# A graph network's joined node pass: ScalarE's copy of turned rows moved between the halves of the next item's normalization, and TensorE's product behind the base product

## The chip, the cores and the metric

The kernel runs on one core of a Trainium2 chip. The metric is the device time of one execution in microseconds, the median of a few runs. The core has TensorE (PE, matrix products into PSUM), VectorE (DVE), ScalarE (ACT), GpSimd (POOL) and SyncE (SP); DMAs are issued here from SP, ScalarE and GpSimd and run on 16 DMA engines. Each engine runs its own program in order, and the programs meet only at semaphores.

## What is computed

There are 100000 nodes of 128 features and 50000 edges, sorted by their destination. Two residual blocks follow each other, each on `relu(layernorm(x))`:

```
h = relu(layernorm(x))
x = x + relational_conv(h)          # 16 relations out of 8 bases, summed over the edges into dst, + h_bias
h = relu(layernorm(x))
g = leaky(h @ enc_w + enc_b)        # leaky(v) = v or 0.1 v
for l in 0, 1:
    agg = segment_sum(g[src], dst) / max(degree, 1)
    g = leaky(agg @ lin_l_w[l] + lin_l_b[l] + g @ lin_r_w[l])
x = x + g
```

All of it is float32.

## The kernel before

The kernel makes four passes, one after the other: a relational pass over the edges, the node pass, and one pass for each of the two layers. The change is in the node pass alone (`node_pass`, L985). It computes the new `x`, its layer norm, the encoder's `g`, and of layer 0 the two parts that need no exchange between nodes: the base `g @ w_r + bias` for every node, and for every edge the row of `g` at its source, summed over equal destinations within the sorted edges and multiplied by `w_l`.

The pass walks 294 items, in a repeating order of three: two blocks of 512 nodes and one tile of 512 edges. For edges the rows of `x` at the source come from a copy that the pass before laid out by edge, and the rows of the aggregate are gathered with indirect DMAs. I call three items a beat; there are 98.

One item goes through these steps:
- SP loads `first` and `term` (L1106 to L1110) into a ring of 12 slots. GpSimd gathers `term` for edges (L1075) and scatters the finished rows (L1084), each with four indirect DMAs a beat.
- VectorE adds the two (L1299), takes statistics (L1304) and, once a beat, the variance of 12 groups (L1314 to L1324). ScalarE takes the square root, `deviation` (L1233). VectorE makes `rstd` and `shift` from it (L1332, L1334).
- ScalarE normalizes with `normalize(n, lo, hi)` (L1244): four instructions of 128 columns, called in two halves, (0, 2) and (2, 4). Only the second half signals that `h` is complete.
- TensorE turns the four 128x128 pieces (`turn`, L1158) into a PSUM bank; ScalarE copies the turned rows to SBUF (`keep_turned`, L1254).
- TensorE multiplies by `enc_w` (`product`): for a block one product that leaves features on the partitions (L1179), for edges the bias and four products (L1171, L1175).
- ScalarE makes a tenth of the product (`tenth`, L1264 for blocks, L1261 for edges), and VectorE takes the maximum of product and tenth (`leaky`, L1349 for blocks, L1343 for edges).
- For blocks TensorE computes the base (`base_product`, L1187 and L1191), ScalarE evicts it (`keep_base`, L1271), and SP stores it (L1130). For edges TensorE sums runs (`sum_runs`, L1202), VectorE carries the sums on (L1380), TensorE multiplies by `w_l` (`to_rows`, L1211) and VectorE scales the rows (`finish`, L1389).

The order of the work is written out by hand, as one loop over n on each engine, in which each step works at an item some places back. The lag of a step is the same on both sides of the change. `ht_ps`, `g_ps`, `z_ps`, `h`, `ht`, `tmp` and `g_t` have two buffers each. The waits that matter here: `keep_turned(n)` waits for `turn(n)`; `product(n)` waits for `keep_turned(n)` and for the maximum of item n-2, whose bank it takes; `tenth(n)` waits for `product(n)`; `base_product(n)` and `sum_runs` wait for the maximum of their item; `keep_base` waits for its base product; `turn(n)` waits for the second half of `normalize(n)`.

In iteration n TensorE has this order: product of item n-1, run sums or base product of item n-3, row product of item n-5 (if it is a tile of edges), turn of item n. ScalarE has: the deviation if a beat is about to begin, copy of n-1, tenth of n-2, first half of the normalization of n, base eviction of n-4 (if it is a block), second half of n. VectorE has: carried sums of n-4, addition and statistics of n+4, the variance, the scales of the next beat, the maximum of n-2, and the comparisons and the scaling of rows for edges.

Of the kernel before, what the change touches and what calls it, by code (L numbers as in the profile page):

```python
# [68 lines left out]
def gnn_kernel(nc, x, src, dst, etype, basis_w, w_comp, h_bias, enc_w, enc_b, lin_l_w, lin_l_b,  # L69
# [20 lines left out]
    with ctx:  # L90
# [894 lines left out]
        def node_pass():  # L985

            X_TILES = 4
            ITEMS = 3 * (T // X_TILES)
# [7 lines left out]
            with ExitStack() as st:  # L996
# [54 lines left out]
                def block_of(n):  # L1051
                    return n // 3 * 2 + n % 3

                def valid(n, edges):
                    return 0 <= n < ITEMS and is_edges(n) == edges
# [9 lines left out]
                with nc.Block() as block:  # L1065
# [85 lines left out]
                    @block.tensor  # L1151
                    def _(pe):
                        def turn(n):
                            pe.wait_ge(s_h, n + 1)
                            if n >= 2:
                                pe.wait_ge(s_ht, n - 1)
                            for j in range(NB):
                                last = nc.tensor.transpose(ht_ps[n % 2][:, j * P:(j + 1) * P],  # L1158
                                                           h[:, n % 2, j * P:(j + 1) * P], ident[:])
                            last.then_inc(s_turn, 1)  # L1160

                        def wait_g_bank(n):

                            if n >= 0:
                                pe.wait_ge(s_leaky, n + 1)

                        def product(n):
                            pe.wait_ge(s_ht, n + 1)
                            wait_g_bank(n - 2)
                            if is_edges(n):  # L1170
                                nc.tensor.matmul(g_ps[n % 2][:], ones_bf[0:96, :],  # L1171
                                                 bias_parts[0:96, 0, :].unsqueeze(1).to_broadcast([96, NB, P]),
                                                 start=True, stop=False)
                                for j in range(NB):
                                    last = nc.tensor.matmul(g_ps[n % 2][:, j * P:(j + 1) * P],  # L1175
                                                            ht[:, n % 2, j * P:(j + 1) * P], w_enc[:],
                                                            start=False, stop=(j == NB - 1))
                            else:
                                last = nc.tensor.matmul(g_ps[n % 2][:], w_enc[:], ht[:, n % 2, :], start=True, stop=True)  # L1179
                            last.then_inc(s_g, 1)  # L1180

                        def base_product(n):
                            d = block_of(n)
                            pe.wait_ge(s_leaky, n + 1)
                            if d >= 2:
                                pe.wait_ge(s_kept, d - 1)
                            nc.tensor.matmul(z_ps[d % 2][:], ones_bf[0:96, :],  # L1187
                                             bias_parts[0:96, 1, :].unsqueeze(1).to_broadcast([96, NB, P]),
                                             start=True, stop=False)
                            for j in range(NB):  # L1190
                                last = nc.tensor.matmul(z_ps[d % 2][:, j * P:(j + 1) * P],  # L1191
                                                        g_t[:, d % 2, j * P:(j + 1) * P], w_r[:, 0, :],
                                                        start=False, stop=(j == NB - 1))
                            last.then_inc(s_z, 1)

                        def sum_runs(i):
                            pe.wait_ge(s_leaky, 3 * i + 3)
                            pe.wait_ge(s_same, i + 1)
                            if i:
                                pe.wait_ge(s_carried, i * X_TILES)  # L1200
                            for j in range(X_TILES):
                                last = nc.tensor.matmul(sum_ps[:, j * P:(j + 1) * P], g_rows[:, i % 2, j * P:(j + 1) * P],  # L1202
                                                        same[:, i % 2, j, :], start=True, stop=True)
                            last.then_inc(s_summed, 1)

                        def to_rows(i):
                            pe.wait_ge(s_carried, (i + 1) * X_TILES)
                            if i:
                                pe.wait_ge(s_rows, i)
                            for j in range(X_TILES):  # L1210
                                last = nc.tensor.matmul(row_ps[:, j * P:(j + 1) * P], sums[:, j, :], w_l[:, 0, :],  # L1211
                                                        start=True, stop=True)
                            last.then_inc(s_rowed, 1)

                        for n in range(ITEMS + 6):
                            if 1 <= n <= ITEMS:
                                product(n - 1)
                            if valid(n - 3, True):
                                sum_runs((n - 3) // 3)
                            if valid(n - 3, False):  # L1220
                                base_product(n - 3)
                            if valid(n - 5, True):
                                to_rows((n - 5) // 3)
                            if n < ITEMS:
                                turn(n)

                    @block.scalar
                    def _(act):
                        def deviation(b):
                            act.wait_ge(s_var, b + 1)  # L1230
                            if b >= 2:
                                act.wait_ge(s_rstd, b - 1)
                            nc.scalar.activation(std[:, b % 2, :], var[:, b % 2, :], ACT.Sqrt).then_inc(s_std, 1)  # L1233

                        def normalize(n, lo, hi):
                            b, k = n // 3, n % 3
                            if lo == 0:
                                act.wait_ge(s_shift, b + 1)
                                act.wait_ge(s_base, n + 1)
                                if n >= 2:  # L1240
                                    act.wait_ge(s_turn, n - 1)
                            for j in range(lo, hi):
                                c = k * NB + j
                                last = nc.scalar.activation(h[:, n % 2, j * P:(j + 1) * P],  # L1244
                                                            base[:, n % SLOTS, j * P:(j + 1) * P], ACT.Relu,
                                                            bias=shift[:, b % 2, c:c + 1], scale=rstd[:, b % 2, c:c + 1])
                            if hi == NB:
                                last.then_inc(s_h, 1)
# [7 lines left out]
                        def tenth(n):  # L1256
                            act.wait_ge(s_g, n + 1)
                            if n >= 2:
                                act.wait_ge(s_leaky, n - 1)
                            if is_edges(n):  # L1260
                                nc.scalar.activation(tmp[:, n % 2, :], g_ps[n % 2][:], ACT.Copy,  # L1261
                                                     scale=SLOPE).then_inc(s_tenth, 1)
                            else:
                                nc.scalar.activation(tmp[:, n % 2, :], g_ps[n % 2][:], ACT.Identity, bias=tenth_col[:],  # L1264
                                                     scale=SLOPE).then_inc(s_tenth, 1)
# [8 lines left out]
                        for n in range(-1, ITEMS + 4):  # L1274
                            if (n + 1) % 3 == 0 and n + 1 < ITEMS:
                                deviation((n + 1) // 3)
                            if 1 <= n <= ITEMS:
                                keep_turned(n - 1)
                            if 0 <= n - 2 < ITEMS:
                                tenth(n - 2)  # L1280
                            if 0 <= n < ITEMS:
                                normalize(n, 0, 2)
                            if valid(n - 4, False):
                                keep_base(block_of(n - 4))
                            if 0 <= n < ITEMS:
                                normalize(n, 2, NB)

# [670 lines left out]
```

## Time and profile before

| | us |
|---|---|
| median of 3 runs | 3753.05 (3751.85 to 3756.4) |
| the profiled execution, its own time | 3751.84 |
| its span, first to last instruction | 3749.7 |
| VectorE busy | 3011.4 (80%) |
| GpSimd busy | 2473.7 (66%) |
| TensorE matmuls busy | 2432.4 (65%) |
| ScalarE busy | 1879.4 (50%) |
| mean granted clock of TensorE | 0.894 of full |

The profile is of one execution. The normalization instructions of the node pass start between 1239.4 and 2384.8 us, so this pass takes a bit under a third of the span. In the rows below "idle before" in brackets is how long the engine stood before the instruction, and behind the arrow is what released it. A PE line is a matrix product, PEld the loading of its weights. The end of a matrix product is modelled. Durations of neighbouring instructions on one engine overlap, so the distance from start to start is the better price of an instruction.

### The profile page before, as it was taken

The page shows a single profiled execution, that of the slowest core. Times are in us where ns is not written, and L with a number is a line of the kernel's source. Part 1 is how long each engine was busy: PE and PEld are TensorE (multiplying, and loading weights), DVE is VectorE, ACT ScalarE, POOL GpSimd, SP SyncE. Part 2 cuts the span into 40 slices and gives each one's busy share as a digit, 9 for nine tenths or more (in the row PEclk, how much of TensorE's full clock was granted, in tenths as well). Part 3 has the DMA queues.
Part 4 walks back from the last instruction along what each step waited for, and adds up shares of the span by engine and source line. Part 5 has one row for each costly group of instructions (what it writes and reads, how often), then busy time and mean ns, then how long its engine had stood idle before and what let it go on. Part 6 is the DMA issues. An engine that isn't in the chain of part 4 may idle for free. (4 is left out here: it accounts for less than half of the span.)

```text
span 3749.7 us, 58608 instructions
## 1 busy us (share of the span) xinstructions
PE 2432.4 (65%) x13938; PEld 1774.0 (47%) x13938; DVE 3011.4 (80%) x8321; ACT 1879.4 (50%) x4979; POOL 2473.7 (66%) x2363
## 2 busy tenths in 40 slices
PE   1679999999998577777777777477778871000000
PEld 0445555555554466665565566377777771000000
DVE  3479999999998788888888888688888884555565
ACT  0346666666665577777777777345445541000000
POOL 0357777777776567666666666576666654677665
PEclk9989999999999899999999999799999995555555
DMA  8776666666662888888888888399999997999998
GB/s 277 312 235 205 203 201 209 206 209 207 208 198 65 274 254 259 262 263 265 265 265 266 268 267 249 133 346 388 389 383 385 388 370 300 416 416 416 415 410 319
DMA packets 664350, 1065.77 MB, mean 284 GB/s; under 512 B 74065, under 2 KB 379651, under 8 KB 657586
## 3 DMA queue, kind: packets, MB, share of 16 engines
q1 hardware_dynamic: 486572, 599.67, 49.5%
q10 hardware_dynamic: 95904, 305.70, 20.4%
q0 software_dynamic: 81536, 156.64, 13.0%
q8 instruction: 121, 1.98, 0.2%
q14 instruction: 217, 1.78, 0.1%
HBM read 596.92 MB, written 488.74 MB: 290 GB/s over the span
## 5 line engine op out<-in xcount | busy, mean ns | idle before, releaser
L946 PE MATMUL y_ps_rel<-w_basis,ht_rel 128*128 128x512 f32 x1568 | 753.6, 604 | 57.5 <-DVE two_rel L815 57.2
L1694 POOL DMA_INDIRECT gat_l<-base_and_means,src_c x392 | 457.6, 1167 | 211.3 <-DVE act_gat_l L1801 107.2
L1084 POOL DMA_INDIRECT base_and_means<-rows_node,odd_c x392 | 398.0, 1015 | 269.0 <-DVE rows_node L1389 162.9
L1699 POOL DMA_INDIRECT means<-late_l,put_c x392 | 419.8, 1071 | 235.5 <-DMA late_l<-means_by_edge 120.1
L668 POOL DMA_INDIRECT gat_rel<-in_x_dram,src_c x392 | 404.2, 1031 | 157.0 <-issue 79.3
L1244 ACT ACTIVATE h_node<-base_node,shift_node,rstd_node 128x128 f32<-128x128 f32 x1176 | 502.4, 489 | 1.6 <-DVE shift_node L1334 1.6
L677 POOL DMA_INDIRECT agg<-rows_rel,put_c x392 | 400.3, 1021 | 134.6 <-issue 104.2
L1075 POOL DMA_INDIRECT term_node<-agg,src_c x392 | 391.5, 999 | 128.3 <-issue 119.6
L815 DVE SCALAR_TENSOR_TENSOR two_rel<-y_ps_rel,coef,two_rel 128x128 f32<-128x128 f32 x1568 | 438.8, 343 | 0.0
L946 PEld LDWEIGHTS y_ps_rel<-w_basis,ht_rel 128*128 128x128 f32 x1568 | 265.4, 192 | 268.6 <-issue 171.0
L1624 DVE TENSOR_TENSOR last_z_l<-last_z_l,node_done_l 128x1024 f32<-128x1024 f32 x98 | 120.3, 1227 | 272.2 <-DMA node_done_l<-means 272.2
L957 PEld LDWEIGHTS sum_ps_rel<-same_rel,two_rel 128*128 128x128 f32 x1568 | 237.7, 192 | 188.6 <-issue 120.3
L885 ACT ACTIVATE part_rel<-y_ps_rel,coef 128x128 f32<-128x128 f32 x784 | 241.7, 360 | 138.2 <-PE y_ps_rel L946 117.0
L1179 PE MATMUL g_ps_node<-ht_node,w_enc 128*128 128x512 f32 x392 | 222.6, 650 | 134.5 <-ACT ht_node L1254 134.5
L1254 ACT ACTIVATE ht_node<-ht_ps_node 128x512 f32<-128x512 f32 x294 | 175.5, 597 | 259.9 <-PE ht_ps_node L1158 259.9
L1899 PE MATMUL sum_ps_l<-same_l,act_gat_l 128*128 128x128 f32 x784 | 167.6, 297 | 154.0 <-DVE act_gat_l L1804 119.2
L1304 DVE BATCH_NORM_STATS2 st_node<-base_node 128x6 f32<-128x128 f32 x1176 | 256.5, 281 | 10.2
L1541 ACT ACTIVATE ht_l<-ht_ps_l 128x512 f32<-128x512 f32 x196 | 116.9, 596 | 265.4 <-PE ht_ps_l L1533 226.9
L815 DVE SCALAR_TENSOR_TENSOR two_rel<-y_ps_rel,coef,part_rel 128x128 f32<-128x128 f32 x784 | 236.9, 344 | 11.4 <-ACT part_rel L885 11.1
L957 PE MATMUL sum_ps_rel<-same_rel,two_rel 128*128 128x128 f32 x1568 | 238.8, 275 | 0.6 <-DVE sums_rel L827 0.6
L1158 PE MATMUL ht_ps_node<-ident,h_node 128*128 128x128 f32 x1176 | 183.4, 279 | 84.9 <-ACT h_node L1244 84.9
L1349 DVE SCALAR_TENSOR_TENSOR g_t_node<-g_ps_node,enc_col,tmp_node 128x512 f32<-128x512 f32 x196 | 145.6, 743 | 101.2 <-ACT tmp_node L1264 101.2
(167 smaller groups left out, 6030.7 us busy)
## 6 DMA issues: line engine op xcount, KB each, us to landing
pairs_l<-base_and_means SPq DMA_DIRECT2D x196, 512.0 KB, 7.2
base_and_means<-zero_row SPq DMA_DIRECT2D x49, 1024.0 KB
means<-zero_row SPq DMA_DIRECT2D x49, 1024.0 KB
first_node<-in_x_dram SPq DMA_DIRECT2D x196, 256.0 KB, 2.7
term_node<-agg SPq DMA_DIRECT2D x196, 256.0 KB, 3.4
x<-base_node SPq DMA_DIRECT2D x196, 256.0 KB, 4.4
base_and_means<-done_node SPq DMA_DIRECT2D x196, 256.0 KB
z<-node_done_l ACTq DMA_DIRECT2D x196, 256.0 KB, 7.4
```

Of the source, the lines that this page charges most:

```text
L668: nc.gpsimd.indirect_dma_start(gat[:, g, j, :], None, x, bass.IndirectOffsetOnAxis(ap=src_c[:, t:t + 1], axis=0)).then_inc(s_gathered[g][j ...
L677: nc.gpsimd.indirect_dma_start(agg, bass.IndirectOffsetOnAxis(ap=put_c[:, t:t + 1], axis=0), rows[:, q, j, :], None, bounds_check=N - 1, o ...
L815: nc.vector.scalar_tensor_tensor(acc[:, a, :], y[:, b * P:(b + 1) * P], c, prior, ALU.mult, ALU.add).then_inc(s_acc, 1)
L885: last = nc.scalar.activation(part[:, s, a, :], y_ps[s][:, b * P:(b + 1) * P], ACT.Copy, scale=coef[:, bass.ds(m * HALF + j, 1), b])
L946: nc.tensor.matmul(y_ps[(q + j) % 2][:, c * 512:(c + 1) * 512], ht[:, q, j, :], w_basis[:, 4 * c:4 * c + 4, :], start=True, stop=True).the ...
L957: last = nc.tensor.matmul(sum_ps[s][:, 0:P], two[:, j, a, :], same[:, q, j, :], start=(a == 0), stop=(a == 1))
L1075: nc.gpsimd.indirect_dma_start(term[:, q, j * P:(j + 1) * P], None, agg, bass.IndirectOffsetOnAxis(ap=src_c[:, t:t + 1], axis=0)).then_inc ...
L1084: nc.gpsimd.indirect_dma_start(pair.rearrange("n (k f) -> (n k) f", k=2), bass.IndirectOffsetOnAxis(ap=odd_c[:, t:t + 1], axis=0), rows[:, ...
L1244: last = nc.scalar.activation(h[:, n % 2, j * P:(j + 1) * P], base[:, n % SLOTS, j * P:(j + 1) * P], ACT.Relu, bias=shift[:, b % 2, c:c + ...
L1304: nc.vector.bn_stats(st6[:, n // 3 % 2, n % 3, j, :], base[:, n % SLOTS, j * P:(j + 1) * P]).then_inc(s_stat, 1)
L1694: nc.gpsimd.indirect_dma_start(gat[:, q, j, :], None, source, bass.IndirectOffsetOnAxis(ap=src_c[:, t:t + 1], axis=0)).then_inc(s_gathered ...
L1699: nc.gpsimd.indirect_dma_start(means1, bass.IndirectOffsetOnAxis(ap=put_c[:, t:t + 1], axis=0), rows_, None, bounds_check=N - 1, oob_is_er ...
```

## The change

Two loops get another order; no step is changed in itself. In TensorE's loop the product of item n-1 is issued behind the run sums or the base product of item n-3. In ScalarE's loop the tenth of n-2 and the base eviction of n-4 come first, then the first half of the normalization of n, then the copy of the turned rows of n-1, then the second half.

```diff
                         for n in range(ITEMS + 6):
-                            if 1 <= n <= ITEMS:
-                                product(n - 1)
                             if valid(n - 3, True):
                                 sum_runs((n - 3) // 3)
                             if valid(n - 3, False):
                                 base_product(n - 3)
+                            if 1 <= n <= ITEMS:
+                                product(n - 1)
                             if valid(n - 5, True):
                                 to_rows((n - 5) // 3)
                             if n < ITEMS:
...
                         for n in range(-1, ITEMS + 4):
                             if (n + 1) % 3 == 0 and n + 1 < ITEMS:
                                 deviation((n + 1) // 3)
+                            if 0 <= n - 2 < ITEMS:
+                                tenth(n - 2)
+                            if valid(n - 4, False):
+                                keep_base(block_of(n - 4))
+                            if 0 <= n < ITEMS:
+                                normalize(n, 0, 2)
                             if 1 <= n <= ITEMS:
                                 keep_turned(n - 1)
-                            if 0 <= n - 2 < ITEMS:
-                                tenth(n - 2)
-                            if 0 <= n < ITEMS:
-                                normalize(n, 0, 2)
-                            if valid(n - 4, False):
-                                keep_base(block_of(n - 4))
                             if 0 <= n < ITEMS:
                                 normalize(n, 2, NB)
```

## Rows read from the trace of the kernel before

**Rows 1.** The page's head and busy times over the whole span.
```profile
span 3749.7 us, 58608 instructions
...
PE 2432.4 (65%) x13938; PEld 1774.0 (47%) x13938; DVE 3011.4 (80%) x8321; ACT 1879.4 (50%) x4979; POOL 2473.7 (66%) x2363
```

**Rows 2.** Three stretches: length; busy PE, PEld, DVE, ACT, POOL; PEclk; DMA share; GB/s.
```profile
1200.00:1300.00 100.00, 55.21 (x295) 38.85 (x294) 63.65 (x210) 51.64 (x128) 51.95 (x52) 0.78 0.68 232
...
1800.00:1900.00 100.00, 77.22 (x501) 59.78 (x502) 89.63 (x277) 77.44 (x180) 69.44 (x71) 1.00 0.89 267
...
2500.00:2600.00 100.00, 80.71 (x616) 74.86 (x617) 88.11 (x150) 49.41 (x116) 66.77 (x60) 0.97 1.01 382
```

**Rows 3.** Waits of VectorE and ScalarE, 1300 to 2350 us: total, times, longest.
```profile
DVE g_t_node L1349 <- ACT tmp_node L1264: 86.0, 90, 1.0
...
ACT ht_node L1254 <- PE ht_ps_node L1158: 235.4, 269, 1.1
```

**Rows 4.** Timeline of a beat, VectorE: start, length, line, what it writes and reads.
```profile
1806.47 0.17 DVE L1324 SCALAR_TENSOR_TENSOR var_node<-within_node,square_node 128x12 f32<-128x12 f32 x1
...
1808.91 0.17 DVE L1334 SCALAR_TENSOR_TENSOR shift_node<-mean_node,rstd_node 128x12 f32<-128x12 f32 x1
...
1810.04 0.75 DVE L1349 SCALAR_TENSOR_TENSOR g_t_node<-g_ps_node,enc_col,tmp_node 128x512 f32<-128x512 f32 x1 [0.96 <-ACT tmp_node L1264]
...
1821.74 0.75 DVE L1349 SCALAR_TENSOR_TENSOR g_t_node<-g_ps_node,enc_col,tmp_node 128x512 f32<-128x512 f32 x1 [0.96 <-ACT tmp_node L1264]
```

**Rows 5.** Timeline of the same beat, ScalarE and TensorE.
```profile
1804.58 0.60 ACT L1254 ACTIVATE ht_node<-ht_ps_node 128x512 f32<-128x512 f32 x1 [0.82 <-PE ht_ps_node L1158]
...
1805.08 0.59 ACT L1261 ACTIVATE tmp_node<-g_ps_node 128x512 f32<-128x512 f32 x1
...
1805.23 1.12 PE L1179 MATMUL g_ps_node<-ht_node,w_enc 128*128 128x512 f32 x2 [0.69 <-ACT ht_node L1254]
...
1805.55 0.87 ACT L1244 ACTIVATE h_node<-base_node,shift_node,rstd_node 128x128 f32<-128x128 f32 x2
...
1806.19 0.38 PE L1187 MATMUL z_ps_node<-bias_parts,ones_bf 96*128 96x512 bf16 x1
...
1806.32 0.59 ACT L1271 ACTIVATE done_node<-z_ps_node 128x512 f32<-128x512 f32 x1
1806.41 1.05 PE L1191 MATMUL z_ps_node<-w_r,g_t_node 128*128 128x128 f32 x8
...
1806.80 0.87 ACT L1244 ACTIVATE h_node<-base_node,shift_node,rstd_node 128x128 f32<-128x128 f32 x2
...
1807.31 1.06 PE L1211 MATMUL row_ps_node<-w_l,sums_node 128*128 128x128 f32 x8
...
1808.20 0.60 PE L1158 MATMUL ht_ps_node<-ident,h_node 128*128 128x128 f32 x4
...
1808.84 0.60 ACT L1254 ACTIVATE ht_node<-ht_ps_node 128x512 f32<-128x512 f32 x1 [1.06 <-PE ht_ps_node L1158]
...
1809.33 0.68 ACT L1264 ACTIVATE tmp_node<-g_ps_node,tenth_col 128x512 f32<-128x512 f32 x1
...
1809.90 0.87 ACT L1244 ACTIVATE h_node<-base_node,shift_node,rstd_node 128x128 f32<-128x128 f32 x2
```

**Rows 6.** Timeline in the pass's drain: a tenth that waits for its product.
```profile
2386.72 0.39 PE L1171 MATMUL g_ps_node<-bias_parts,ones_bf 96*128 96x512 bf16 x1 [0.69 <-ACT ht_node L1254]
...
2388.03 0.60 ACT L1261 ACTIVATE tmp_node<-g_ps_node 128x512 f32<-128x512 f32 x1 [0.80 <-PE g_ps_node L1175]
```

**Rows 7.** Timeline at the start of the pass: a product at the lower clock.
```profile
1246.47 2.07 PE L1179 MATMUL g_ps_node<-ht_node,w_enc 128*128 128x512 f32 x2 [0.69 <-ACT ht_node L1254]
```

**Rows 8.** GpSimd's indirect DMAs: both groups (busy, mean ns, idle before), and one in the drain.
```profile
L1084 POOL DMA_INDIRECT base_and_means<-rows_node,odd_c x392 | 398.0, 1015 | 269.0 <-DVE rows_node L1389 162.9 <-issue 106.0
L1075 POOL DMA_INDIRECT term_node<-agg,src_c x392 | 391.5, 999 | 128.3 <-issue 119.6 <-POOLq L554 8.8
...
2375.65 0.98 POOL L1084 DMA_INDIRECT base_and_means<-rows_node,odd_c  x1 [0.30 <-issue]
```

## The prediction

> **What bounds the kernel now.** I read the page's totals first: the profiled execution has a span of 3749.7 us, and its own time is 3751.84 us, 1.2 us under the median of 3753.05; the sum below is made against 3751.84 and 1.2 is added at the end. VectorE is the busiest engine over the whole span, with 80% [rows 1]. The busy times by stretch then show the node pass, some 1240 to 2400 us: in its middle VectorE is busy 89.6 of 100 us, TensorE 77, ScalarE 77, GpSimd 69, and the DMA engines have a share of 0.89 [rows 2]. So VectorE is nearly, but not quite, the bound there, and the question is what its missing tenth waits for. The waits answer: from 1300 to 2350 us VectorE waits 90 times, 86.0 us in all, for ScalarE's tenth (L1264), which the maximum of L1349 needs; ScalarE in the same stretch waits 269 times, 235.4 us, for TensorE's turn (L1158) before it can copy the turned rows (L1254) [rows 3].
>
> The timeline gives the period. The maximum that waits 0.96 us for its tenth starts at 1810.04 and again, with the same wait, at 1821.74: 11.70 us for a beat of three items (two blocks, one tile of edges) [rows 4]. There are 294 items, so 98 beats, 1147 us. Of a beat VectorE works, with the gaps between its instructions, 11.70 - 0.96 = 10.74 us. That is the floor that a new order of ScalarE and TensorE cannot go below.
>
> What sets 11.70 is a loop between two engines. TensorE turns (1808.20), ScalarE copies (1808.84), TensorE multiplies (the like step: copy at 1804.58, product at 1805.23), then the base product (from 1806.19), the row product (1807.31), and only then the next turn (1808.20) [rows 5]. While the copy runs TensorE has nothing to do, since the product stands first in its iteration; while the turn runs ScalarE has nothing to do, since the copy stands first in its.
>
> **The change, part by part.** No instruction is added or removed and nothing moves on SP, GpSimd or VectorE; in this pass neither of the two issues a DMA. Two programs get another order.
>
> *TensorE*: run sums or base product now stand ahead of the product, so they run while ScalarE still works at the halves of the normalization and the copy. The turn then follows the product directly (once in a beat behind the row product), and the base product falls out of the loop. The added danger is that the product is queued behind a base product that waits for a maximum (L1349 or L1343); it is priced below.
>
> *ScalarE*: tenth, base eviction, first half, copy, second half. The copy no longer waits for the turn, which has had a tenth, an eviction and half a normalization to finish. Instead the tenth may wait for the product. I call K the start of the copy and work out the distance to the next K. The product starts 0.65 after the copy (1804.58 to 1805.23), takes 1.12, and ScalarE starts about 0.04 later, so a tenth of a block can start at K + 1.81 [rows 5]. For a tile of edges the drain of the pass shows the wait itself: product at 2386.72, tenth at 2388.03, 1.31 us, so K + 1.96 [rows 6]. ScalarE is free before that: copy 0.50 (1804.58 to 1805.08) and half a normalization 0.77 (1805.55 to 1806.32) end at K + 1.27; the deviation, 0.2 us, fits into what is left. From the tenth on, ScalarE's own starts count: tenth of a block 0.57 (1809.33 to 1809.90), of edges 0.47 (1805.08 to 1805.55), base eviction 0.48 (1806.32 to 1806.80), half 0.77 [rows 5]. The three distances:
> - tenth of a block, no eviction: 1.81 + 0.57 + 0.77 = 3.15
> - tenth of edges, eviction: 1.96 + 0.47 + 0.48 + 0.77 = 3.68
> - tenth of a block, eviction: 1.81 + 0.57 + 0.48 + 0.77 = 3.63
>
> Together 10.46 us a beat, against 10.74 of VectorE. The new loop is the shorter by 0.28, so VectorE becomes the bound.
>
> *Does TensorE keep up?* Its fullest item is the one with the row product: product pitch 0.96 (1805.23 to 1806.19), row product 0.89 (1807.31 to 1808.20), turn 0.60, then run sums or base product, for which I take 1.12 (1806.19 to 1807.31) [rows 5]. From K + 0.65 that ends at K + 4.22; the next product is due at K + 3.63 + 0.65 = K + 4.28. It just fits. The turn is done at K + 3.10, before the next K at + 3.63.
>
> *Does VectorE deliver in time?* The base product needs the maximum of its item, and the product of two items later is queued behind it. The circle is tenth 0.7, maximum 0.75, base product 0.38 + 1.05 at most, product 1.12, signals 0.1: 4.1 us, and it goes round once in two items, for which 2/3 of 10.74, 7.2 us, are there. So 3.1 us are left for a VectorE that comes late to its maximum. The deviation needs the variance, ready at 1806.64, and the shift is ready at 1809.08, 2.44 later [rows 4]; ScalarE needs the shift one item after its deviation, 3.6 later. No circle through VectorE is longer than its own 10.74.
>
> *What is queued behind the new waits?* Behind a tenth that waits for its product stand ScalarE's eviction, a half and the copy, for which TensorE waits; that is in the three distances. The base eviction comes half a normalization earlier in its iteration, so SP's store of it (L1130) and the loads queued behind that store can only start earlier.
>
> *The sum*: 98 beats x 0.96 = 94 us is the most. I take 90, that is 10.78 a beat, since two other resources come near. The DMA engines work 0.89 x 11.70 = 10.4 us a beat, a share of 0.97 at 10.74; the last layer's pass shows 1.01 [rows 2], so there is room. GpSimd has eight indirect DMAs a beat, four of 1.00 and four of 1.015 us, with 0.30 between them: (0.999 + 1.015) x 4 + 8 x 0.30 = 10.46 [rows 8]. 3751.84 - 90 = 3662, plus 1.2: 3663 us. Bounds of what is not seen in the trace: DMA at a share near 1 may cost nothing, or hold VectorE until a beat of 11.0; a wait of the tenth on the product may cost 0.03 (as seen) or 0.25 more each, which makes 10.46 into 11.2. That leaves 0.7 and 0.5 a beat, 69 and 49 us. I take the near ends: for the DMA because loads are issued twelve items ahead, for the wait because rows 6 show it directly.
>
> **A rule against it.** Scatters in the pass's drain, where VectorE is often idle, take 0.98 us; in the full pass their mean is 1.015 [rows 8]. A fuller VectorE can thus hardly cost GpSimd more than 0.04 on each of eight, 0.3 us a beat. The Trainium skill (SBUF — State Buffer, on who interferes with whom) says that a VectorE instruction with two SBUF inputs shares a port with a GpSimd instruction that reads SBUF, and that the second to issue blocks until the first is done. By that rule GpSimd would be stretched as VectorE loses its last pauses, and would come out as the bound. Its result is rival 2, priced from the rows.
>
> **Rivals.**
> 1. *DMA or latency of the new loop holds the beat at 10.9 to 11.3.* For it: DMA share 0.97, and three waits on a product instead of three on a turn. Against: 1.01 is reached elsewhere, and the wait is in rows 6. At 11.1: 98 x 0.60 = 59 us, 3694.
> 2. *GpSimd becomes the bound.* It has 0.28 us of room. With 0.04 more on each instruction, 10.46 + 0.32 = 10.78: nothing lost to speak of; with 0.08, 11.10: 3694 again. For it: the closeness. Against: with VectorE at 0.9 the price is 0.035 already.
> 3. *No change:* a DMA ceiling near its present share. The beat would stay at 11.6 or more, 3743 to 3753. The higher share in rows 2 speaks against it.
> 4. *Slower: the product stands behind a late base product.* The place is TensorE's queue: if the maximum that the base product waits for comes less than 1.3 us before the copy ends, round after round, TensorE runs base product after the copy and puts it back into the loop, now behind a ScalarE chain that is longer than before. All three times 1.12 gives 10.46 + 3.36 = 13.8 a beat, +207 us, 3960; it is slower than before once more than 1.24 us a beat are lost so. It decides at maxima over 3.1 us later than their tenths allow. TensorE's clock would do the like: before the pass has warmed up a product takes 2.07 instead of 1.13 [rows 7], where the granted clock was 0.78 and TensorE was 55% busy; three times 0.94 more makes 13.3. But in the pass it is granted in full at 77% busy, and will be busy 84%.
>
> **How the numbers follow.** VectorE as the bound, 10.72 to 10.90 a beat: 0.74, with 3656 to 3674 as its own range. Rivals 1 and 2 together 0.17, rival 3 0.04, rival 4 0.05. The range from 3654 (more than 96 us won, ends of the pass included) to 3700 takes in the first two rivals up to a beat of 11.15 or so. About 0.2% (7.5 us) is what a measurement of this kernel can tell; faster by more than that is 0.91, the same 0.04, slower 0.05.
>
> **What would show it.** Right: beats of 10.75 to 10.80, ScalarE's wait for L1158 gone, in its place short waits of tenths for L1175 or L1179; VectorE's wait of 0.96 for L1264 gone; its busy time near 97 of 100 us in the pass; TensorE's pause before each product shortened, some 84 busy. The node pass ends about 90 us earlier and what follows is as long as before. Wrong: if VectorE waits for first_node or term_node loads (rival 1 or 3), if GpSimd's waits for rows_node vanish and VectorE waits for gathered rows (rival 2), or if the product waits with its copy long done (rival 4).

## The result and the profile after

The changed kernel takes 3650.28 us (median of 4 runs, 3649.98 to 3657.83), against 3754.73 us before (median of 4): a ratio of 0.9727, 95% interval 0.9710 to 0.9744, 102 us or 2.7% faster. The forecast was 3663 us in a range from 3654 to 3700. Direction and mechanism are as forecast; the time lies 4 us below the range, and the step behind that is a small and instructive one.

The profiled execution takes 3649.98 us, 101.9 less than the one before. First the profile page's head and busy times, which answer to [rows 1]:

```profile
span 3647.9 us, 58608 instructions
...
PE 2424.6 (66%) x13938; PEld 1782.1 (49%) x13938; DVE 3003.6 (82%) x8321; ACT 1879.7 (52%) x4979; POOL 2495.0 (68%) x2363
```

VectorE, ScalarE and TensorE work as long as before, within 8 us, and GpSimd 21 us longer; it is the waiting that shrank. The stretches that answer to [rows 2], with the same columns:

```profile
1800.00:1900.00 100.00, 84.25 (x554) 66.76 (x553) 96.82 (x302) 84.89 (x198) 77.21 (x75) 1.00 0.96 290
...
2400.00:2500.00 100.00, 79.88 (x622) 74.11 (x623) 89.09 (x153) 49.99 (x117) 67.59 (x60) 0.98 1.01 381
```

VectorE went from 89.6 to 96.8 busy, TensorE from 77 to 84, GpSimd from 69 to 77, and the DMA share from 0.89 to 0.96 (in the next pass it is 1.01 as before). What each engine waits for in the node pass, 1300 to 2250 us, answers to [rows 3] (total us, times, longest). VectorE, ScalarE and GpSimd:

```profile
DVE g_t_node L1349 <- issue: 0.3, 1, 0.3
DVE g_rows_node L1343 <- issue: 0.3, 1, 0.3
...
ACT tmp_node L1261 <- PE g_ps_node L1175: 54.0, 89, 0.6
ACT std_node L1233 <- DVE var_node L1324: 45.0, 85, 0.9
ACT tmp_node L1264 <- PE g_ps_node L1179: 42.0, 94, 0.5
...
POOL base_and_means L1084 <- issue: 112.3, 356, 1.7
POOL term_node L1075 <- issue: 107.7, 353, 0.3
POOL term_node L1075 <- DVE base_node L1299: 0.6, 2, 0.3
```

GpSimd in the kernel before, 1300 to 2350 us, for comparison:

```profile
POOL base_and_means L1084 <- DVE rows_node L1389: 117.5, 73, 1.6
```

VectorE no longer waits for a tenth: 86.0 us are gone. ScalarE's 235.4 us for the turn are gone too; in their place stand short waits of the tenths for their products. New is that ScalarE waits for VectorE's variance, that is, it runs ahead of VectorE now. GpSimd, which used to wait 117.5 us for rows_node, shows hardly anything but its own issue, so by this view it is a second candidate for the bound.

The timeline of VectorE around the beat's start answers to [rows 4]:

```profile
1802.92 0.17 DVE L1334 SCALAR_TENSOR_TENSOR shift_node<-mean_node,rstd_node 128x12 f32<-128x12 f32 x1
...
1803.01 0.75 DVE L1349 SCALAR_TENSOR_TENSOR g_t_node<-g_ps_node,enc_col,tmp_node 128x512 f32<-128x512 f32 x1
...
1813.68 0.75 DVE L1349 SCALAR_TENSOR_TENSOR g_t_node<-g_ps_node,enc_col,tmp_node 128x512 f32<-128x512 f32 x1
```

From maximum to maximum it is 10.67 us, where it was 11.70. And the maximum starts 0.09 after the *start* of the shift, 0.08 before the shift has ended. Before, it started 1810.04 - 1808.91 = 1.13 after it. The beat lost 1.13 - 0.09 = 1.04 us, although the row said that the engine was idle for 0.96.

ScalarE's timeline answers to [rows 5]: the copy, and the tenth that waits for its product, of a block and of a tile of edges.

```profile
1802.62 0.58 ACT L1254 ACTIVATE ht_node<-ht_ps_node 128x512 f32<-128x512 f32 x1
...
1804.42 0.69 ACT L1264 ACTIVATE tmp_node<-g_ps_node,tenth_col 128x512 f32<-128x512 f32 x1 [0.45 <-PE g_ps_node L1179]
...
1805.78 0.58 ACT L1254 ACTIVATE ht_node<-ht_ps_node 128x512 f32<-128x512 f32 x1
...
1807.73 0.60 ACT L1261 ACTIVATE tmp_node<-g_ps_node 128x512 f32<-128x512 f32 x1 [0.60 <-PE g_ps_node L1175]
```

The first and the last start of L1244, 1242.7 and 2283.7 us, give 1041.0 us for the normalizations, where it was 1145.4 before: 104.4 less, of which the beat is 98 x 1.03 = 101. The pass starts 3.3 us later than in the execution before, so that 101.9 are left. That start differs from execution to execution, from 1237 to 1251 us in those profiled beside kernels before of 3751 to 3755 us, so the last 3 us aren't to be read as part of the effect.

### The profile page after: what moved, and what is told of

Read it like the earlier page. It is cut to its first block and busy times, and to the rows that moved or that the text cites. A ratio compares the mean times of both kernels' runs of the same rounds, so it can differ in the third digit from the quotient of the medians.

```text
span 3647.9 us, 58608 instructions
## 1 busy us (share of the span) xinstructions
PE 2424.6 (66%) x13938; PEld 1782.1 (49%) x13938; DVE 3003.6 (82%) x8321; ACT 1879.7 (52%) x4979; POOL 2495.0 (68%) x2363
## 5 line engine op out<-in xcount | busy, mean ns | idle before, releaser
L1084 POOL DMA_INDIRECT base_and_means<-rows_node,odd_c x392 | 423.1, 1079 | 149.7 <-issue 122.3
L1244 ACT ACTIVATE h_node<-base_node,shift_node,rstd_node 128x128 f32<-128x128 f32 x1176 | 512.1, 488 | 1.6 <-DVE shift_node L1334 1.6
L1075 POOL DMA_INDIRECT term_node<-agg,src_c x392 | 380.2, 970 | 128.0 <-issue 118.7
L1304 DVE BATCH_NORM_STATS2 st_node<-base_node 128x6 f32<-128x128 f32 x1176 | 256.5, 281 | 10.2
L1551 PEld LDWEIGHTS z_ps_l<-w_r,ht_l 128*128 128x128 f32 x1568 | 214.6, 198 | 8.5
L1551 PE MATMUL z_ps_l<-w_r,ht_l 128*128 128x128 f32 x1568 | 214.0, 281 | 0.0
L1191 PEld LDWEIGHTS z_ps_node<-w_r,g_t_node 128*128 128x128 f32 x1568 | 207.2, 192 | 6.5
```

The lines of the kernel that those rows point to most:

```text
L1075: nc.gpsimd.indirect_dma_start(term[:, q, j * P:(j + 1) * P], None, agg, bass.IndirectOffsetOnAxis(ap=src_c[:, t:t + 1], axis=0)).then_inc ...
L1084: nc.gpsimd.indirect_dma_start(pair.rearrange("n (k f) -> (n k) f", k=2), bass.IndirectOffsetOnAxis(ap=odd_c[:, t:t + 1], axis=0), rows[:, ...
L1304: nc.vector.bn_stats(st6[:, n // 3 % 2, n % 3, j, :], base[:, n % SLOTS, j * P:(j + 1) * P]).then_inc(s_stat, 1)
L1551: last = nc.tensor.matmul(z_ps[c % 2][:, j * P:(j + 1) * P], ht[:, c % 2, j * P:(j + 1) * P], w_r[:, w.layer, :], start=False, stop=(j == ...
```

## The experiments

The experiments ran in four series, each with the kernel before beside it. In the first and the third the kernel before took 4521 and 4417 us instead of some 3755 (the last section comes back to that), so their ratios are given, but the beats are read from the second and the fourth series.

**TensorE's order alone.** Before, with

```diff
+                            if valid(n - 3, True):
+                                sum_runs((n - 3) // 3)
+                            if valid(n - 3, False):
+                                base_product(n - 3)
                             if 1 <= n <= ITEMS:
                                 product(n - 1)
-                            if valid(n - 3, True):
-                                sum_runs((n - 3) // 3)
-                            if valid(n - 3, False):
-                                base_product(n - 3)
```

> Before, with TensorE's new order alone; ScalarE still copies first. Theory A (the gain is the loop copy-product-base product-turn opened, and VectorE becomes the bound only when both engines are reordered): TensorE's part of the loop goes, ScalarE's serial chain copy, tenth, half, eviction, half, then turn, stays: about 3.9, 3.8 and 3.4 us for the three items, some 11.1 to 11.2 a beat, 50 us faster than before, with VectorE still waiting some 0.5 us a beat for a tenth. Theory B (TensorE's order alone carries the gain, ScalarE's is idle decoration): beat 10.67, 102 us faster.

> TensorE's new order alone, once more, because the kernel before took 4521 us instead of 3755 in the first series, with stalls of ScalarE and TensorE that the profile puts down to issue or to nothing on the core. Where the kernel before takes its 3755 us, theory A gives 11.1 to 11.2 us a beat, 50 us faster than before; theory B 10.67, 102 us faster. Where it takes 4500, the ratio is again near 0.984.

Measured: 0.9838 (0.9801 to 0.9875) in the first series; in the second 3702.01 against 3754.39 us, 0.9855 (0.9838 to 0.9871), 52 us faster. The timeline of that run, VectorE's maximum in two successive beats:

```profile
1803.48 0.75 DVE L1349 SCALAR_TENSOR_TENSOR g_t_node<-g_ps_node,enc_col,tmp_node 128x512 f32<-128x512 f32 x1 [0.47 <-ACT tmp_node L1264]
...
1814.70 0.75 DVE L1349 SCALAR_TENSOR_TENSOR g_t_node<-g_ps_node,enc_col,tmp_node 128x512 f32<-128x512 f32 x1 [0.48 <-ACT tmp_node L1264]
```

The beat is 11.22 us, and half of VectorE's wait remains. That is theory A's number; theory B (this order alone carries the whole gain) is out.

**ScalarE's order alone.** Before, with the ScalarE part of the change only.

> Before, with ScalarE's new order alone; TensorE still has the product ahead of the base product. Theory A: turned copy to turn still holds product, base product or run sums, and once the row product; with the tenth behind the product the three items take about 3.7, 4.4 and 3.4 us, some 11.5 a beat, 20 us faster than before. Theory C (ScalarE's order alone carries the gain): beat 10.67, 102 us faster. If it is slower than before, the two parts need each other.

> ScalarE's new order alone, once more. Where the kernel before takes its 3755 us: theory A 11.5 us a beat, 20 us faster; theory C 10.67, 102 us faster. Where it takes 4500, no gain again.

Measured: 1.0054 (1.0000 to 1.0109) and, in the second series, 3756.5 against 3754.39 us, 1.0010 (1.0000 to 1.0019). No gain; the 20 us that I had expected are not there. Its waits from 1600 to 2200 us (51 beats), VectorE's and ScalarE's:

```profile
DVE sums_node L1380 <- PE sum_ps_node L1202: 50.4, 52, 1.0
...
ACT done_node L1271 <- PE z_ps_node L1191: 47.5, 102, 0.5
ACT tmp_node L1261 <- PE g_ps_node L1175: 30.9, 51, 0.6
ACT tmp_node L1264 <- PE g_ps_node L1179: 23.6, 52, 0.5
```

One wait had been left out. With TensorE's old order the base product runs after the product; ScalarE takes the tenth of that product at once and then wants to evict the very base product that has just begun. It stands for it 0.47 us in the mean, twice a beat, with the half and the copy behind it. The copies start at 1800.91, 1805.23, 1809.47 and 1812.64 us: 4.32, 4.24 and 3.17 us, where the expectation had 3.7, 4.4 and 3.4. The eviction's wait stands in the first (0.51) and in the second (0.42); it is the first, behind a tenth of edges, that came out longer than expected, and the beat is 11.73. VectorE's wait has only changed its name, from the tenth to the run sums. With both orders changed the base product is long done when the eviction comes: in the changed kernel the wait for L1191 is absent. So the parts are worth 52 and 0 us alone and 102 together. Theory C (this order alone carries the gain) is out as well.

**The copy ahead of both halves.** The changed kernel, with

```diff
+                            if 1 <= n <= ITEMS:
+                                keep_turned(n - 1)
                             if 0 <= n < ITEMS:
                                 normalize(n, 0, 2)
-                            if 1 <= n <= ITEMS:
-                                keep_turned(n - 1)
```

> The changed kernel, with the copy ahead of both halves (tenth, base eviction, copy, first half, second half). ScalarE's chain from copy to copy then has no half in it but the product's latency: about 3.1, 3.0 and 2.9 us, 9.0 a beat instead of 10.46. Theory A (VectorE is the bound at 10.67): no change against the changed kernel, 101 us faster than before, only ScalarE's waits move. Theory D (the new ScalarE-TensorE loop, near 10.5, still sets or shares the beat): 10 us or more faster than the changed kernel.

> The changed kernel with the copy ahead of both halves, once more. Theory A (VectorE is the bound): beat 10.67, 101 us faster than before, equal to the changed kernel's ratio of 0.973. Theory D (the ScalarE-TensorE loop still sets or shares the beat): 10 us or more beyond it, 0.970 or less.

> The changed kernel itself, beside the others on the same chip. Where the kernel before takes 3755 us: ratio 0.973, beat 10.67. Where it takes 4500: about 0.977, as the copy ahead of both halves did.

Measured in the first series 0.9769 (0.9735 to 0.9803). In the second 3647.55 us, 0.9712 (0.9696 to 0.9728), beside the changed kernel's 3650.58, 0.9721 (0.9704 to 0.9737): the same within the intervals. That its loop between ScalarE and TensorE is shorter shows only in the lighter version further down (undisturbed beats of 10.14 against 10.49 us). Here ScalarE waits for no product any more, but longer for VectorE's variance, 73.8 us instead of the 30.5 of the changed kernel in this series, between 1600 and 2200 us:

```profile
ACT std_node L1233 <- DVE var_node L1324: 73.8, 56, 1.7
ACT ht_node L1254 <- PE ht_ps_node L1158: 9.7, 57, 0.2
```

Theory D is out: the loop doesn't bind in the changed kernel. The place between the halves is not what makes the change work; that the copy comes after tenth and eviction, and TensorE has other work meanwhile, is enough.

**Is it VectorE or GpSimd?** Two edits take work from one of them each. The first takes it from VectorE:

```diff
+                            w = P if i < 2 else 8
+                            k = X_TILES if i < 2 else 1
-                            nc.vector.tensor_tensor(open_[:, i % 2, :, :], columns(i),
-                                                    last_before.to_broadcast([P, X_TILES, P]),
+                            nc.vector.tensor_tensor(open_[:, i % 2, 0:k, 0:w], columns(i)[:, 0:k, 0:w],
+                                                    last_before[:, 0:k, :].to_broadcast([P, k, w]),
                                                     ALU.is_equal).then_inc(s_open, 1)
```

The second takes two scatters of four from GpSimd, with the counts of their semaphore to match:

```diff
-                            for j in range(X_TILES):
+                            for j in range(X_TILES if i < 3 else 2):
                                 t = i * X_TILES + j
                                 nc.gpsimd.indirect_dma_start(
                                     pair.rearrange("n (k f) -> (n k) f", k=2),
```

> The changed kernel with the comparison of L1368 cut from 512 to 8 columns from the third tile of edges on (it leaves out most of the mask that carries sums on), which takes some 0.5 us a beat off VectorE: 10.16 instead of 10.66. Theory A (VectorE is the bound, and the ScalarE-TensorE loop of the changed order, 10.46, is next): beat 10.4 to 10.5, 15 to 25 us faster than the changed kernel. Theory E (GpSimd is already the bound at 10.67, since it shows no wait in the changed kernel): no change.

> The light comparison in the changed kernel once more, since the kernel before took 4417 us in that series. Where it takes 3755 us: theory A (VectorE was the bound, the ScalarE-TensorE loop at 10.46 is next) beat 10.4 to 10.5, 15 to 25 us faster than the changed kernel, ratio to before 0.966 to 0.968; theory E (GpSimd is already the bound) 10.67, ratio 0.972.

Measured 0.9894 (0.9857 to 0.9931) in the third series; in the fourth 3632.59 against 3750.89 us, 0.9681 (0.9662 to 0.9699), some 15 us faster than the changed kernel's ratios of 0.9727 and 0.9721 would give (it did not run in this series). The first line is VectorE's wait from 1600 to 2200 us; the others are ScalarE's timeline of that run, one beat of copies and the tenths that wait:

```profile
DVE g_t_node L1349 <- ACT tmp_node L1264: 15.9, 57, 0.3
...
1500.65 0.58 ACT L1254 ACTIVATE ht_node<-ht_ps_node 128x512 f32<-128x512 f32 x1
...
1502.60 0.60 ACT L1261 ACTIVATE tmp_node<-g_ps_node 128x512 f32<-128x512 f32 x1 [0.60 <-PE g_ps_node L1175]
...
1504.34 0.59 ACT L1254 ACTIVATE ht_node<-ht_ps_node 128x512 f32<-128x512 f32 x1
...
1506.15 0.69 ACT L1264 ACTIVATE tmp_node<-g_ps_node,tenth_col 128x512 f32<-128x512 f32 x1 [0.35 <-PE g_ps_node L1179]
...
1507.98 0.59 ACT L1254 ACTIVATE ht_node<-ht_ps_node 128x512 f32<-128x512 f32 x1
...
1509.79 0.69 ACT L1264 ACTIVATE tmp_node<-g_ps_node,tenth_col 128x512 f32<-128x512 f32 x1 [0.46 <-PE g_ps_node L1179]
...
1511.14 0.58 ACT L1254 ACTIVATE ht_node<-ht_ps_node 128x512 f32<-128x512 f32 x1
```

From copy to copy 3.69, 3.64 and 3.16 us, together 10.49; the prediction had worked out 3.68, 3.63 and 3.15. VectorE waits once a beat for a tenth again, so the loop is now the bound. GpSimd keeps pace at 10.49 too and waits for nothing, so it can run faster than 10.67. But this edit doesn't separate the two engines cleanly, since a shorter comparison on VectorE can also shorten GpSimd's DMAs (the lengths are shown with the rivals, further down). The half scatters do.

> The same light comparison, with the copy ahead of both halves, whose loop is short (9.0 us). Theory A: the beat falls until GpSimd or VectorE holds it; GpSimd's eight DMAs at their undisturbed 0.98 and 0.94 to 1.0 with 0.30 between give 10.2 to 10.4, VectorE 10.16. So 10.2 to 10.4, 25 to 45 us faster than the changed kernel. Theory E: no change, 10.66.

> The light comparison with the copy ahead of both halves, once more. Where the kernel before takes 3755 us: theory A beat 10.2 to 10.4, ratio to before 0.960 to 0.966; theory E 10.66, ratio 0.972.

Measured 0.9887 (0.9834 to 0.9939), and in the fourth series 3619.92 us, 0.9650 (0.9634 to 0.9666). In an undisturbed beat the maxima are 10.14 us apart (1501.59 and 1511.73), which is VectorE's own work. From 1600 to 2200 us the DMA share is 0.97, GpSimd waits almost only for issue, and VectorE waits at the addition of L1299, with no releaser that the profile names:

```profile
DVE base_node L1299 <- issue: 20.9, 26, 2.3
```

The mean beat from 1300 to 2250 us is 10.48, above the 10.2 to 10.4 that was expected. All these waits are at the addition of a tile of edges, the item whose `term` GpSimd gathers, and none at a block. So at some 10.5 us a beat that tile's data come late: GpSimd's issue of the gathers, the DMAs behind it, or SP's load of the same tile. Which of them holds VectorE was not tried.

> The changed kernel with half of its scatters left out, where the kernel before takes its 3755 us. Theory A: beat 10.66 to 10.67 as in the changed kernel, GpSimd waits 2.6 us a beat, and only the drain is shorter, up to 13 us. Theory E (GpSimd is the bound): beat 10.56 or less.

> The changed kernel with half of its scatters, once more. Where the kernel before takes 3755 us: theory A beat 10.66 to 10.67 and up to 13 us less in the drain; theory E beat 10.56 or less.

Measured 0.9313 (0.9264 to 0.9361) in the third series; the same kernel had 0.9290 (0.9255 to 0.9326) in the first, for which was expected:

> The changed kernel with two scatters a beat instead of four from the fourth tile of edges on (it leaves out half of the rows' scatters, and layer 0's means of these nodes with them). Theory A (VectorE's 10.67 us of own work is the bound): the beat stays at 10.67 and the pass as long, apart from its drain, which is up to 13 us shorter since half of the last scatters go; GpSimd waits some 2.6 us a beat again. Theory E (GpSimd, which in the changed kernel shows no wait but issue, is the bound): the beat falls by 0.1 us or more.

In the fourth series it takes 3643.9 us, 0.9718 (0.9701 to 0.9735), which is the changed kernel's ratio (0.9727 and 0.9721). GpSimd's timeline of it:

```profile
1802.18 1.01 POOL L1084 DMA_INDIRECT base_and_means<-rows_node,odd_c  x1 [3.10 <-DVE rows_node L1389]
1803.49 1.01 POOL L1084 DMA_INDIRECT base_and_means<-rows_node,odd_c  x1 [0.30 <-issue]
1804.81 0.99 POOL L1075 DMA_INDIRECT term_node<-agg,src_c  x1 [0.30 <-issue]
```

GpSimd has 3.1 us of pause in a beat, and the maxima still stand 10.66 us apart (1500.10 and 1510.76), 10.68 in the mean from 1300 to 2250. Theory E is out where the kernel before takes its 3755 us: VectorE sets the beat, and GpSimd's full row of instructions in the changed kernel doesn't. From the last start of L1244 to the end it is 8 us less than in the changed kernel (1356 against 1364), which fits the shorter drain that was expected.

With both edits and the copy ahead of both halves:

> As before it, and with two scatters a beat instead of four (it leaves out the mask and half of the scatters). VectorE's 10.16 is then the only thing near: beat 10.15 to 10.2, and up to 13 us less in the drain. If the beat stays above 10.3, neither VectorE nor GpSimd nor the loop holds it, and the DMA engines are left.

It ran in the third series alone: 0.9381 (0.9309 to 0.9453), no better than half the scatters by themselves (0.9313). Its question, what is left at 10.2, stays open.

**A version that is faster than both.** From this follows a kernel with nothing left out: the copy ahead of both halves, and the mask of L1368 made by ScalarE, which the short loop leaves time for. The destinations are sorted whole numbers, so `d == last` is `relu(last + 1 - d)`. The diff shows the main lines only; the calls of `open_run` on ScalarE, and the addition's place one item earlier in VectorE's loop, are not in it:

```diff
+                        def open_run(i, lo, hi):
...
+                            for j in range(lo, hi):
+                                last = nc.scalar.activation(open_[:, i % 2, j, :],
+                                                            dst_b[:, i % 2, 1 + j * P:1 + (j + 1) * P], ACT.Relu,
+                                                            bias=past[:, i % 2, j:j + 1], scale=-1.0)
...
+                            nc.vector.tensor_scalar(past[:, i % 2, :], last_before, 1.0, None, ALU.add).then_inc(s_past, 1)
```

> A whole kernel: copy ahead of both halves, and the mask of L1368 made by ScalarE, relu(last + 1 - d) in four pieces, with one small addition left to VectorE. VectorE 10.16 a beat, ScalarE's own work 8.84 + 1.54 = 10.4, GpSimd 10.2 to 10.4. Theory A: beat 10.4 to 10.5, ratio to before 0.964 to 0.968, faster than the changed kernel by 15 to 25 us. Theory E: 10.66, no gain against the changed kernel.

Measured: 3621.26 against 3750.89 us, 0.9654 (0.9625 to 0.9684), some 26 us under what the changed kernel's two ratios give. It matches the light comparison with the copy first (0.9650), so ScalarE's four more activations a beat cost nothing that shows. Between 1600 and 2200 us VectorE again waits 19.5 us at that addition (L1316 in this kernel), with a DMA share of 0.96.

## Why the prediction was wrong, and where it was right

*The step that failed* is the floor: "Of a beat VectorE works, with the gaps between its instructions, 11.70 - 0.96 = 10.74 us." The bracket of [rows 4] counts idle time from the end of the instruction before. VectorE's instructions overlap: an undisturbed maximum starts 0.09 us after the start of the shift, while the shift takes 0.17. A wait costs from start to start, 1.13 - 0.09 = 1.04, not 0.96. The term was too small by 0.08 a beat, 98 x 0.08 = 8 us. The text ahead of the prediction says itself that the distance from start to start is the better price; it was used for ScalarE and TensorE, and not for VectorE. The runs show 10.66 to 10.67 in the place of 10.74.

*The second term that failed* is the allowance of 4 us (94 cut to 90) for DMA and GpSimd standing near. It was worth nothing: the DMA share did go to 0.96 and GpSimd to a full row, and VectorE waited for neither (0.6 us of issue in 950). 90 + 4 + 8 = 102. That this meets the measured 101.9 to the tenth is partly luck: the beats alone give 101, and the pass's ends and its later start (104.4 - 3.3) happen to fill the rest. The low end of the range, 3654, was built on the same floor (the prediction calls it 96 us won; from 3753 it is 99). With the floor 8 us lower it would have been some 3646, and the measured 3650 inside.

*What held.* The period of 11.70 and its reason; that the loop would go and VectorE become the bound. The new loop, 10.46 forecast, showed itself at 10.49 as soon as VectorE was lighter, in all three of its distances. TensorE kept up and VectorE came in time: no product stood behind a late maximum so that the beat felt it, though TensorE does wait 38.1 us in 950 for the maximum at L1187. Busy shares of 97 and 84 were forecast, 96.8 and 84.3 measured.

*The rivals.* Rival 1 (DMA or latency at 10.9 to 11.3) didn't come: the tenths start 1.80 and 1.95 us after the copy, where 1.81 and 1.96 were worked out. Rival 2 (GpSimd) was near. Over the whole run its scatters rose from 1.015 to 1.079 us and its gathers fell from 0.999 to 0.970. Within the pass its load isn't constant: from 1300 to 1400 us they take 1.013 and 0.981 and the first scatter still waits for its rows (0.57 before it, where its own issue takes 0.30), from 1750 to 2200 us 1.092 and 0.964, and it has no pause left:

```profile
1302.77 0.69 DVE L1389 TENSOR_TENSOR rows_node<-row_ps_node,inv_c 128x512 f32<-128x512 f32 x1
...
1304.26 1.01 POOL L1084 DMA_INDIRECT base_and_means<-rows_node,odd_c  x1 [0.57 <-issue]
...
1804.28 0.68 DVE L1389 TENSOR_TENSOR rows_node<-row_ps_node,inv_c 128x512 f32<-128x512 f32 x1
...
1808.09 1.02 POOL L1084 DMA_INDIRECT base_and_means<-rows_node,odd_c  x1 [0.30 <-issue]
```

The scatters rose by 0.08, twice the 0.04 that the prediction held possible for one DMA, but with the shorter gathers the eight rose by 0.25 a beat, within its 0.3. The half scatters show that GpSimd didn't bind. Rivals 3 and 4 didn't come; TensorE's granted clock stayed at 1.00.

*The rule of the Trainium skill* (SBUF — State Buffer, who interferes with whom) can be looked at now. It speaks of VectorE instructions with two SBUF inputs against GpSimd instructions that read SBUF. Whether the issue of an indirect DMA is such a one, no run here shows; of the first kind in this pass are the addition (L1299) and the two comparisons (L1359, L1368), each 0.68 us long. In the changed kernel, between 1400 and 2200 us, 110 of some 600 indirect DMAs on GpSimd start 0.36 to 0.38 us after the start of an addition and take 1.185 us in the mean; 20 start 0.16 to 0.19 us after that of a comparison of L1368 and take 1.38 to 1.41 (one 2.01); those that start over 0.5 us after such a start take 0.94 to 1.02. In the kernel before, seven start 0.02 or 0.03 us after a comparison of L1368 and take 1.53 or 1.54 (one 2.14).

```profile
1402.87 0.68 DVE L1368 TENSOR_TENSOR open_node<-dst_b_node 128x512 f32<-128x512 f32 x1
...
1403.06 1.38 POOL L1084 DMA_INDIRECT base_and_means<-rows_node,odd_c  x1 [0.30 <-issue]
...
1809.04 0.68 DVE L1299 TENSOR_TENSOR base_node<-first_node,term_node 128x512 f32<-128x512 f32 x1
...
1809.41 1.20 POOL L1084 DMA_INDIRECT base_and_means<-rows_node,odd_c  x1 [0.30 <-issue]
...
1810.91 0.99 POOL L1084 DMA_INDIRECT base_and_means<-rows_node,odd_c  x1 [0.30 <-issue]
```

The earlier in such an instruction a DMA starts, the longer it takes: over 0.98, it is 0.56, 0.42 and 0.20 us more where 0.65, 0.51 and 0.31 us of the instruction are left. So the trace goes with the rule. VectorE's addition keeps its length (0.682 us before, 0.683 after). What the rule would have made of the beat, GpSimd as the bound, did not come: it is 0.2 to 0.4 us on one or two DMAs of eight. That the port is the cause was not tried by itself; the times only fit it.

*In the experiments* two expectations missed: in ScalarE's order alone, the wait of the eviction for its base product was left out, and in the light comparison with the copy ahead of both halves the mean beat was 10.48, not 10.2 to 10.4.

## What to carry to other kernels

When a wait on the bounding engine is priced, take it from start to start of the two instructions and subtract their undisturbed distance; the idle time in brackets leaves out the overlap that the wait destroyed, 0.08 of 1.04 us here. Where two in-order engines hand an item back and forth, reorder both or work out both: one order alone gave half the gain, the other none, since the wait only moved to the next hand-over. And an engine without a pause isn't thereby the bound: take work from each of the two full engines in turn and see which one the period follows, and look whether the work taken from one also lightens the other.

## What the runs showed that I had not expected

In two of the four series every kernel was much slower: before 4521 and 4417 us instead of 3751 to 3755. Both ran on one and the same chip, the second and fourth on two others. In the node pass of the kernel with the copy ahead of both halves (first series) VectorE and GpSimd instructions take their usual times, but ScalarE and TensorE stand for microseconds, with a releaser that is not on the core:

```profile
2110.52 0.69 ACT L1264 ACTIVATE tmp_node<-g_ps_node,tenth_col 128x512 f32<-128x512 f32 x1 [3.91 <-remote]
...
2111.24 0.75 DVE L1349 SCALAR_TENSOR_TENSOR g_t_node<-g_ps_node,enc_col,tmp_node 128x512 f32<-128x512 f32 x1 [4.17 <-ACT tmp_node L1264]
```

Nearly every beat has such a stall: of 77 beats between 1550 and 2750 us four are under 11.2 us, and the median is 15.2. The DMA share is lower, 0.66 at 199 GB/s (1700 to 2700 us) against 0.96 at 290 in the changed kernel, and TensorE's granted clock is 0.85 from 1600 to 2200 us, where it was 1.00. The changed kernel itself did not run in these two series. Its version with the copy ahead of both halves gains 2.3% (0.9769); with the lighter comparison, in the third series, it is 1.1%. With half of the scatters the kernel is 5% faster than the copy-first one of the same series (4193.9 against 4409.1 us), an edit that does nothing on the other chips. It isn't GpSimd's time that is short there: in the copy-first kernel it waits 199.7 of 600 us for its rows. What stalls the engines was neither seen nor tried; that it has to do with the traffic of the small scatters is a guess.
